# Row-tiled max scores, rounds of eight heads in the second pass, and a ring of two for the route weights of the last experts

## Chip, cores and metric

One core of one Trainium2 chip runs the whole program. The metric is the device time in microseconds (us) of one execution; three executions are shown for the kernel before, and one more was profiled.

## The reference

The program is a two-layer Perceiver block on x (256 tokens x 512) with a context of 4096 rows x 512. Each layer is cross attention to the context, self attention, and a mixture of experts, each with a residual. The change touches the second layer's cross attention (int8-rounded queries, 16 heads of 32) and its experts (32 experts, 8 per token). What these compute, cut to its core:

```python
# cross attention of layer 1: x -> queries, context -> keys and values
q = qdq(layernorm(x)) @ qdq(wq).T + bq          # 256 x 512, 16 heads of 32
k, v = split(ctx @ wkv.T + bkv)                 # 4096 x 512 each
o = softmax(q k^T / sqrt(32)) v                 # over the 4096 context rows
x = x + qdq(o) @ qdq(wp).T + bp
# experts of layer 1
scores = softmax(x @ wg.T); weights, idx = top_k(scores, 8); weights /= sum(weights)
h = silu(x_e @ w1[e]) * (x_e @ v1[e])           # 32 experts, hidden 192
out[t] += (h @ w2[e]) * weight[t, e]
```

## The kernel before

All tokens stay in SBUF (two tiles of 128 tokens, also kept transposed). The stages run one after the other, each in blocks that all engines enter and leave together; within a block the engines are ordered by semaphores alone, and each engine runs its list in order. Large products are made of three fp32r matmuls (high x high, low x high, high x low; the helper `product3`, L175 to L177).

**Cross attention, first pass** (stage_cross1, L1168 to L1346). The keys and values of the context are computed and the greatest score of each query is found, in 8 chunks k of 512 context rows. The work of TensorE for the next chunk is cut into 8 units (2 halves of 256 rows; in each, w = 0 and 1 make keys with 24 matmuls of 256 columns a unit, w = 2 and 3 make values with 12 matmuls of 512 columns), each unit into 4 quarters. Between two quarters stands one matmul of scores (L1278): for one head h and one tile t of 128 queries, `q_hi[:, h, tile]` (128 rows of which 32 hold the head's queries and 96 are zeros) against `keys_hi[:, u, h // 4, :]` (the keys of four heads on 128 rows), 512 columns, to one of the banks 0 to 3 in turn. VectorE takes the maximum of each (L1340), 32 in a chunk, and between them, at i = 1 and i = 18, splits the next context rows into high and low parts (`split`, L1326 and L1328). The matmul of turn i waits until the reduction four turns earlier is done. The last chunk has the 32 scores and no units. ScalarE takes keys and values out of PSUM (`take`), GpSimd makes the low part of the keys, SyncE stores keys in DRAM and loads context rows.

In the block before, `q_hi` is cleared by GpSimd (L1094) and filled by four copies of VectorE (L1122 to L1125), which are the last of its block; L1214 and the stores go on from `qT_hi` and `qT_lo`, the same queries with the heads of four on 128 rows.

**Second pass** (L1405 to L1532). For each of 32 tiles T of 128 context rows, TensorE makes the scores of 8 pairs p of heads (S, two matmuls a pair, L1513, to bank p % 4), ScalarE the exponentials of a pair (L1473), VectorE adds them up (L1459, pairs 0, 1, 4 to 7; pairs 2 and 3 are summed by TensorE, L1485), TensorE multiplies them with the values four pairs later (V, L1495). TensorE goes in rounds of two pairs: S of pairs p and p+1, then V of pairs p-4 and p-3. S of a pair waits for the exponential that used its bank. Stacked keys `k_stack` come from DRAM in two slots of two tiles each, three DMAs a slot (L1358), issued when the slot's last S is done.

**Experts** (stage_moe1, L1933 to L2198). The 32 experts are 16 pairs k. TensorE's order is up(0), up(1), down(0), up(2), down(1), and so on. The route weights are written to DRAM as 32 rows of 256 tokens and spread to all partitions in three groups of pairs, (0), (1 to 3), (4 to 15), into one tile `weight` of 16 pairs (load_weight, L1990 to L1997). SyncE issues them in one list with the expert weights: group 0, up(2, 0), group 1, up(2, 1), down(1), group 2, and then body(k) with up(k+3, 0), up(k+3, 1) and down(k+2). VectorE's `weigh` (L2154 to L2158) multiplies the hidden values with the weights and waits for the group once.

Of the kernel before, what the change touches and what calls it, by code (L numbers as in the profile page):

```python
# [1038 lines left out]
def stage_cross1(nc, g, A):  # L1039
    with ExitStack() as ctx:  # L1040
# [15 lines left out]
        q_hi = sb("q_hi", [P, Y_H, L], F32R, pass_scope)  # L1056
# [9 lines left out]
        with ExitStack() as c1:  # L1066
# [7 lines left out]
            (wq_loaded, wp_loaded, bias_loaded, pads_cleared, grid_step, x_rounded, wq_rounded,  # L1074
             wp_rounded, x_turned, w_turned, w_copied, x_copied, q_done, q_ready, split) = (sem(n) for n in (
                 "wq_loaded", "wp_loaded", "bias_loaded", "pads_cleared", "grid_step",
# [14 lines left out]
            with nc.Block() as block:  # L1091
                @block.gpsimd
                def _(pool):
                    pool.memset(q_hi[:, :, :].bitcast(F32), 0.0).then_inc(pads_cleared, 1)  # L1094
                    for c in range(NC):
                        kv.rest(pool, c)

                @block.vector
                def _(dve):
# [17 lines left out]
                    dve.wait_ge(pads_cleared, 1)  # L1117
# [54 lines left out]
        with ExitStack() as c2:  # L1172
# [20 lines left out]
            with nc.Block() as block:  # L1193
# [52 lines left out]
                def _(pe):  # L1246
# [40 lines left out]
                def _(act):  # L1287
# [22 lines left out]
                    def body(k, u, prep, more):  # L1310
                        if prep:
                            act.wait_ge(scores_ready, 32 * k + 1)
# [10 lines left out]
                def _(dve):  # L1323
# [7 lines left out]
                    def body(k, u, prep, more):  # L1331
                        for i in range(32):
# [6 lines left out]
                            dve.wait_ge(scores_ready, 32 * k + i + 1)  # L1339
# [62 lines left out]
        with ExitStack() as c4:  # L1402
# [18 lines left out]
            with nc.Block() as block:  # L1421
# [27 lines left out]
                def _(dve):  # L1449
                    def body(T, v, first, prep):  # L1450
                        for p in range(Y_PAIRS):
                            if p in PE_SUMS:
                                continue
                            dve.wait_ge(probs_ready, 8 * T + p + 1 + BANKS)
                            if first:
                                dve.tensor_copy(sums[:, p, :], probs[:, p, :]).then_inc(added, 1)
                                continue
                            dve.wait_ge(added, adds_before(T, p) + 1 - ADDS)
                            dve.tensor_tensor(sums[:, p, :], sums[:, p, :], probs[:, p, :], ALU.add).then_inc(added, 1)  # L1459
# [5 lines left out]
                def _(act):  # L1465
                    def body(T, v, first, prep):
                        for p in range(Y_PAIRS):
                            n = 8 * T + p
                            act.wait_ge(s_ready, n + 1)
                            act.wait_ge(pv_done, n + 1)  # L1470
                            if p not in PE_SUMS:
                                act.wait_ge(added, adds_before(T, p) + 1 - ADDS)
                            act.activation(probs[:, p, :], g.bank[p % BANKS][:, :], ACT.Exp).then_inc(probs_ready, 1)  # L1473
# [5 lines left out]
                def _(pe):  # L1479
# [22 lines left out]
                    def body(T, v, first, prep):  # L1502
# [3 lines left out]
                        for p in range(0, Y_PAIRS, 2):  # L1506

                            n = 8 * T + p
                            for b in range(2):
# [9 lines left out]
                            if p >= LAG or not first:  # L1519
                                pe.wait_ge(probs_ready, n - LAG + 2 + BANKS)  # L1520
                                for b in range(2):
# [410 lines left out]
def stage_moe1(nc, g, A):  # L1932
# [3 lines left out]
    with ExitStack() as ctx:  # L1936
# [15 lines left out]
        weight = sb("weight", [P, PAIRS, FC, L], F32)  # L1952
# [19 lines left out]
        weight_loaded = [sem(f"weight_loaded{n}") for n in range(3)]  # L1972
# [17 lines left out]
        def load_weight(sp, group):  # L1990
            k0, k1 = WEIGHT_GROUPS[group]
            pairs = route_dram[2 * k0:2 * k1, :].rearrange("(k j) n -> k j n", j=2)
            sp.dma_start(weight[:, k0:k1, 0:2, :],  # L1993
                         pairs.unsqueeze(0).to_broadcast([P, k1 - k0, 2, L])).then_inc(weight_loaded[group], 16)
            for j in range(2):
                sp.dma_start(weight[rows_of[j][1], k0:k1, 2, :],  # L1996
                             pairs[:, j, :].unsqueeze(0).to_broadcast([REST, k1 - k0, L])).then_inc(weight_loaded[group], 16)  # L1997

        WEIGHT_GROUPS = ((0, 1), (1, 4), (4, PAIRS))
# [17 lines left out]
        with nc.Block() as block:  # L2017
            @block.sync
            def _(sp):
# [6 lines left out]
                load_weight(sp, 0)  # L2026
                sp.wait_ge(gu_split, 3)
                load_up(sp, 2, 0)
                load_weight(sp, 1)
                sp.wait_ge(gu_split, 4)  # L2030
                load_up(sp, 2, 1)
                sp.wait_ge(dn_split, 1)
                load_down(sp, 1)
                load_weight(sp, 2)
# [310 lines left out]
```

## Time and profile before

| | |
|---|---|
| three executions | 1693.37 us median, 1692.62 to 1693.68 |
| the profiled execution | 1694.95 us, its span 1693.1 us |
| mean granted TensorE clock | 0.953 |
| TensorE matmul busy | 1555.1 us, 92% of the span |
| VectorE busy | 1122.3 us, 66% |
| ScalarE busy | 836.8 us, 49% |
| GpSimd busy | 214.4 us, 13% |

TensorE is busy in nearly every stretch. Busy time of a matmul runs from its issue to its end, and matmuls overlap, so what a matmul costs the queue is read from the distance between two starts, not from its own duration. PEclk is the granted clock as a share of full speed (1.00 is 2.4 GHz, 0.50 is 1.2 GHz).

### The profile page before, as it was taken

Reading aid. Unit: us, or ns where it says so; the run is one execution under the profiler, and the core shown is the slowest. Engines: PE = TensorE matmul, PEld = TensorE weight load, DVE = VectorE, ACT = ScalarE, POOL = GpSimd, SP = SyncE. Lnnn points to the kernel's source line nnn. Section 1 sums busy time; section 2 is a strip of 40 time slices with the busy share of each in tenths; the row PEclk is TensorE's granted clock in tenths of the full one; section 3 lists DMA queues with packets and bytes.
Section 4 is the critical chain, followed back from the end, with each engine's and each line's share of the span. In section 5 each row is a group of like instructions: output and inputs, shape, how many; then the busy total and the mean of one; then the engine's idle time right before and its main releaser. Section 6 shows DMA issues by size and latency. Waiting matters only on the chain. (4 is left out here: it accounts for less than half of the span.)

```text
span 1693.1 us, 35216 instructions
## 1 busy us (share of the span) xinstructions
PE 1555.1 (92%) x12406; PEld 1179.0 (70%) x12406; DVE 1122.3 (66%) x2206; ACT 836.8 (49%) x1429; POOL 214.4 (13%) x161
## 2 busy tenths in 40 slices
PE   5999999999979799999389999969999699869998
PEld 3667776777644499999378888835555455669997
DVE  5766666666524488887748888757776376556664
ACT  2677777777724444434122222228877066344553
POOL 0000000000013223323301111111110034000000
PEclk8999999999989799999689999959999799889999
DMA  3111111111020354442333332247774200485551
GB/s 131 45 37 39 41 38 39 37 37 43 1 106 1 138 180 178 164 165 97 124 87 113 112 111 101 74 88 147 144 144 93 81 1 1 147 279 196 180 187 68
DMA packets 74624, 169.13 MB, mean 100 GB/s; under 512 B 5442, under 2 KB 42098, under 8 KB 70963
## 3 DMA queue, kind: packets, MB, share of 16 engines
q1 hardware_dynamic: 74564, 168.35, 33.0%
q8 instruction: 35, 0.57, 0.1%
q14 instruction: 25, 0.20, 0.0%
HBM read 149.41 MB, written 17.33 MB: 98 GB/s over the span
## 5 line engine op out<-in xcount | busy, mean ns | idle before, releaser
L457 ACT ACTIVATE x_probs<-psum 128x1024 f32<-128x1024 f32 x256 | 248.3, 1022 | 12.9 <-PE psum L340 3.6
L175 PE MATMUL psum<-m_x_hi,m_gu_hi 128*128 128x256 f32 (+1 forms) x816 | 233.7, 286 | 15.3 <-DVE m_h L2152 12.8
L176 PE MATMUL psum<-m_x_hi,m_gu_lo 128*128 128x256 f32 (+1 forms) x816 | 232.6, 285 | 0.0
L177 PE MATMUL psum<-m_x_lo,m_gu_hi 128*128 128x256 f32 (+1 forms) x816 | 232.2, 285 | 0.0
L175 PE MATMUL psum<-x_w_hi,x_ctx_hi 128*128 128x256 f32 (+1 forms) x640 | 208.7, 326 | 10.8 <-DVE x_ctx_lo L484 10.8
L1340 DVE TENSOR_REDUCE x_peaks<-psum 128x512 f32 (+1 forms) x256 | 169.0, 687 | 44.2 <-PE psum L1278 43.9
L176 PE MATMUL psum<-x_w_hi,x_ctx_lo 128*128 128x256 f32 (+1 forms) x640 | 195.0, 305 | 0.0
L177 PE MATMUL psum<-x_w_lo,x_ctx_hi 128*128 128x256 f32 (+1 forms) x640 | 194.6, 304 | 0.0
L175 PEld LDWEIGHTS psum<-x_w_hi,x_ctx_hi 128*128 128x128 f32 x640 | 121.5, 190 | 68.1 <-issue 52.1
L175 PEld LDWEIGHTS psum<-m_x_hi,m_gu_hi 128*128 128x128 f32 (+1 forms) x816 | 153.6, 188 | 18.2 <-DVE m_h L2152 13.4
L1473 ACT ACTIVATE x_probs<-psum 128x512 f32<-128x512 f32 x256 | 138.8, 595 | 34.9 <-PE psum L1513 33.0
L176 PEld LDWEIGHTS psum<-m_x_hi,m_gu_lo 128*128 128x128 f32 (+1 forms) x816 | 153.6, 188 | 1.2
L177 PEld LDWEIGHTS psum<-m_x_lo,m_gu_hi 128*128 128x128 f32 (+1 forms) x816 | 153.7, 188 | 0.0
L1459 DVE TENSOR_TENSOR x_sums<-x_sums,x_probs 128x512 f32<-128x512 f32 x186 | 118.9, 688 | 50.5 <-ACT x_probs L1473 50.5
L349 PE MATMUL psum<-x_probs,x_vals 128*17 128x256 f32 x2048 | 135.4, 382 | 0.0
L176 PEld LDWEIGHTS psum<-x_w_hi,x_ctx_lo 128*128 128x128 f32 x640 | 122.3, 191 | 5.4 <-issue 0.2
L177 PEld LDWEIGHTS psum<-x_w_lo,x_ctx_hi 128*128 128x128 f32 x640 | 122.1, 191 | 5.3
L1829 DVE TENSOR_TENSOR m_gu_lo<-m_gu_raw,m_gu_hi 128x704 fp32r<-128x704 f32 x72 | 105.5, 1489 | 24.8 <-ACT m_gu_hi L1723 24.8
L1513 PEld LDWEIGHTS psum<-x_q_stack,x_k_stack 97*128 97x128 f32 x512 | 70.2, 193 | 63.0 <-ACT x_probs L1473 51.1
L1278 PE MATMUL psum<-x_keys_hi,x_q_hi 128*128 128x512 f32 x256 | 105.6, 429 | 0.9
L1513 PE MATMUL psum<-x_q_stack,x_k_stack 97*128 97x256 f32 x512 | 96.9, 313 | 10.2 <-ACTq L1475 10.2
L519 DVE COPY x_keysT<-psum 128x1024 f16<-128x1024 f16 x64 | 44.2, 690 | 83.4 <-PE psum L330 83.0
(298 smaller groups left out, 3024.7 us busy)
## 6 DMA issues: line engine op xcount, KB each, us to landing
m_gu_raw<-in_m_gu SPq DMA_DIRECT2D x18, 1408.0 KB, 5.9
x_k_stack<-x_keys_dram SPq DMA_DIRECT2D x48, 512.0 KB, 7.3
m_gu_raw<-in_m_gu SPq DMA_DIRECT2D x32, 768.0 KB, 4.1
x_ctx_raw<-in_ctxT SPq DMA_DIRECT2D x64, 256.0 KB, 2.6
m_dn_raw<-in_m_down SPq DMA_DIRECT2D x16, 768.0 KB, 4.1
m_dn_raw<-in_m_down SPq DMA_DIRECT2D x18, 512.0 KB, 3.8
x_ctx_raw<-in_ctxT SPq DMA_DIRECT2D x16, 512.0 KB, 3.8
x_keys_dram<-x_keys_hi SPq DMA_DIRECT2D x16, 512.0 KB, 3.2
```

The lines of the kernel that those rows point to most:

```text
L175: pe.matmul(out, a[0], b[0], start=start, stop=False, skip_group_check=True)
L176: pe.matmul(out, a[1], b[0], start=False, stop=False, skip_group_check=True)
L177: return pe.matmul(out, a[0], b[1], start=False, stop=stop, skip_group_check=True)
L349: last = pe.matmul(acc[grp // 2][32 * q:32 * q + XHD + 1, (grp % 2) * L:(grp % 2 + 1) * L], vals[:, s % 2, 4 * grp + q, :], probs[:, grp, ...
L457: act.activation(probs[:, grp, :], g.psum[:, 2 + 2 * (grp % 2):4 + 2 * (grp % 2), :].rearrange("p b n -> p (b n)"), ACT.Exp).then_inc(prob ...
L519: dve.tensor_copy(keysT[:, s % 2, :, :].rearrange("p a n -> p (a n)"), turn_bank.bitcast(F16)).then_inc(keys_ready, 1)
L1278: pe.matmul(g.bank[i % BANKS][:, :], q_hi[:, h, t * P:(t + 1) * P], keys_hi[:, u, h // 4, :], start=True, stop=True).then_inc(scores_ready, 1)
L1340: dve.tensor_reduce(peaks[:, i % 2, i // 2, bass.ds(k, 1)], g.bank[i % BANKS][:, :], AX, ALU.max).then_inc(scores_read, 1)
L1459: dve.tensor_tensor(sums[:, p, :], sums[:, p, :], probs[:, p, :], ALU.add).then_inc(added, 1)
L1473: act.activation(probs[:, p, :], g.bank[p % BANKS][:, :], ACT.Exp).then_inc(probs_ready, 1)
L1513: last = pe.matmul(g.bank[(p + b) % BANKS][:, a * L:(a + 1) * L], k_stack[0:ROWS, s, h, u * P:(u + 1) * P], q_stack[0:ROWS, h, :], start=T ...
L1829: dve.tensor_tensor(gu_lo[:, u, c, :], gu_raw[:, u, c, :], gu_hi[:, u, c, :].bitcast(F32), ALU.subtract).then_inc(gu_split, 1)
```

## The change

Three edits, in different stages.

1. First pass: a round is now one m (four heads) and one t. Four matmuls of 32 rows each, on partitions 32j to 32j+31 of `qT_hi` and `keys_hi`, write banks 0 to 3; one reduction of 128 x (4 x 512) takes all four. There are 8 rounds in a chunk, each followed by a whole unit, and a round waits for the reduction of the round before it. `q_hi`, its clearing and its four copies are gone. The splits of VectorE stand before rounds 1 and 5.
2. Second pass: rounds of four pairs in place of two; the exponentials and the additions are made for two pairs in one instruction.
3. Experts: `weight` holds two pairs; the rows of pair k are spread by four DMAs into slot k % 2; those of pairs 0 and 1 before up(2, 0) is issued, those of pair k+2 in body(k), after down(k+2) and a wait for the weighing of pair k.

```diff
-                    pool.memset(q_hi[:, :, :].bitcast(F32), 0.0).then_inc(pads_cleared, 1)
...
-                    hi = q_hi[:, :, :].rearrange("p (m j) n -> p m j n", j=4)
-                    for j in range(4):
-                        r = slice(32 * j, 32 * j + 32)
-                        dve.tensor_copy(hi[r, :, j, :], qT_hi[r, :, :])
...
-                        for i in range(2 * UNITS * STEPS):
-                            h, t = i // 2, i % 2
-                            pe.wait_ge(scores_read, 32 * k + i + 1)
-                            pe.matmul(g.bank[i % BANKS][:, :], q_hi[:, h, t * P:(t + 1) * P],
-                                      keys_hi[:, u, h // 4, :], start=True, stop=True).then_inc(scores_ready, 1)
+                        for i in range(NC * NT):
+                            m, t = i // NT, i % NT
+                            pe.wait_ge(scores_read, NC * NT * k + i + 1)
+                            for j in range(BANKS):
+                                rows = slice(32 * j, 32 * j + 32)
+                                last = pe.matmul(g.bank[j], qT_hi[rows, m, t * P:(t + 1) * P], keys_hi[rows, u, m, :],
+                                                 start=True, stop=True)
+                            last.then_inc(scores_ready, 1)
                             if prep:
-                                s, w, quarter = i // 16, i // 4 % 4, i % 4
-                                unit(2 * k + 2 + s, s, w, quarter)
+                                for quarter in range(STEPS):
+                                    unit(2 * k + 2 + i // UNITS, i // UNITS, i % UNITS, quarter)
...
-                            if more and i == 18:
+                            if more and i == 5:
...
-                            dve.tensor_reduce(peaks[:, i % 2, i // 2, bass.ds(k, 1)], g.bank[i % BANKS][:, :], AX,
-                                              ALU.max).then_inc(scores_read, 1)
-
-                    dve.sem_inc(scores_read, BANKS)
+                            dve.tensor_reduce(peaks[:, t, 4 * m:4 * m + 4, bass.ds(k, 1)].rearrange("p h k -> p (h k)"),
+                                              g.psum[:, 0:BANKS, :], AX, ALU.max).then_inc(scores_read, 1)
+
+                    dve.sem_inc(scores_read, 1)
...
-                            dve.tensor_tensor(sums[:, p, :], sums[:, p, :], probs[:, p, :], ALU.add).then_inc(added, 1)
+                            dve.tensor_tensor(sums[:, two, :], sums[:, two, :], probs[:, two, :],
+                                              ALU.add).then_inc(added, 2)
...
-                            act.activation(probs[:, p, :], g.bank[p % BANKS][:, :], ACT.Exp).then_inc(probs_ready, 1)
+                            act.activation(probs[:, p:p + 2, :], g.psum[:, p % BANKS:p % BANKS + 2, :],
+                                           ACT.Exp).then_inc(probs_ready, 2)
...
-                        for p in range(0, Y_PAIRS, 2):
+                        for p in range(0, Y_PAIRS, LAG):
 
                             n = 8 * T + p
-                            for b in range(2):
+                            for b in range(LAG):
                                 pe.wait_ge(probs_ready, n + b + 1)
...
-        weight = sb("weight", [P, PAIRS, FC, L], F32)
+        weight = sb("weight", [P, 2, FC, L], F32)
...
+        def load_weight(sp, k, u):
             for j in range(2):
+                row = route_dram[bass.ds(2 * k + j, 1), :]
+                sp.dma_start(weight[:, u, j, :], row.to_broadcast([P, L])).then_inc(weight_loaded[u], 16)
+                sp.dma_start(weight[rows_of[j][1], u, 2, :],
+                             row.to_broadcast([REST, L])).then_inc(weight_loaded[u], 16)
...
+                load_weight(sp, 0, 0)
+                load_weight(sp, 1, 1)
+                for j in range(2):
+                    sp.wait_ge(gu_split, j + 3)
+                    load_up(sp, 2, j)
                 sp.wait_ge(dn_split, 1)
                 load_down(sp, 1)
-                load_weight(sp, 2)
...
                         load_down(sp, k + 2)
+                        sp.wait_ge(scaled, k + 1)
+                        load_weight(sp, k + 2, u)
```

## Rows read from the trace of the kernel before

**Rows 1.** Windows: engines' busy us (instructions), granted clock, DMA share, GB/s.

```profile
1240.00:1260.00 20.00, 20.00 (x211) 11.17 (x205) 14.38 (x23) 16.06 (x30) 1.94 (x4) 1.00 0.76 143
1510.00:1520.00 10.00, 8.87 (x59) 8.87 (x60) 8.58 (x10) 6.56 (x9) 0.00 (x0) 0.74 0.69 240
1543.00:1556.00 13.00, 13.00 (x94) 12.18 (x93) 8.77 (x10) 6.62 (x8) 0.00 (x0) 1.00 0.52 181
```

**Rows 2.** Timeline, block before the first pass: start, us, engine, work, idle before.

```profile
824.20 3.51 POOL L1094 MEMSET x_q_hi<- 128x4096 f32 x1 [3.94 <-POOLq L89]
825.83 2.55 DVE L1027 TENSOR_SCALAR x_norm<-x_norm,x_per_grid 128x512 f32<-128x512 f32 x2
...
848.94 1.66 DVE L1027 TENSOR_SCALAR x_wp<-x_wp,x_per_grid 128x512 f32<-128x512 f32 x4
...
861.25 2.77 DVE L1125 CAST x_q_hi<-x_qT_hi 32x1024 fp32r<-32x1024 f32 x4
```

**Rows 3.** Timeline of PE in the middle of the first pass.

```profile
956.91 0.40 PE L1278 MATMUL psum<-x_keys_hi,x_q_hi 128*128 128x512 f32 x1
957.15 0.28 PE L175 MATMUL psum<-x_ctx_hi,x_w_hi 128*128 128x256 f32 x1
...
957.86 0.40 PE L1278 MATMUL psum<-x_keys_hi,x_q_hi 128*128 128x512 f32 x1
...
961.78 0.39 PE L175 MATMUL psum<-x_w_hi,x_ctx_hi 128*128 128x512 f32 x1
...
962.46 0.39 PE L1278 MATMUL psum<-x_keys_hi,x_q_hi 128*128 128x512 f32 x1
```

**Rows 4.** Timeline of DVE in the same stretch.

```profile
957.45 0.69 DVE L1340 TENSOR_REDUCE x_peaks<-psum 128x512 f32 x1 [0.26 <-PE psum L1278]
...
967.27 0.69 DVE L1326 CAST x_ctx_hi<-x_ctx_raw 128x1024 fp32r<-128x1024 f32 x1
...
969.13 3.07 DVE L1340 TENSOR_REDUCE x_peaks<-psum 128x512 f32 x5
```

**Rows 5.** Timeline of PE and DVE, last chunk of the first pass.

```profile
1099.52 18.11 PE L1278 MATMUL psum<-x_keys_hi,x_q_hi 128*128 128x512 f32 x32
1099.95 19.22 DVE L1340 TENSOR_REDUCE x_peaks<-psum 128x1 f32<-128x512 f32 x32 [0.22 <-PE psum L1278]
```

**Rows 6.** The line of the max scores: durations ns min/median/max, first and last start.

```profile
L1278 PE MATMUL psum<-x_keys_hi,x_q_hi x256: 387/396/796, 890.5 to 1116.8; 128*128 128x512 f32 x128
```

**Rows 7.** Timeline of PE in the first layer's cross attention, tiles of the array.

```profile
302.35 0.61 PE L340 MATMUL psum<-x_q_rows,x_keysT 64*128 64x256 f16 x8
302.89 1.06 PE L349 MATMUL psum<-x_probs,x_vals 128*17 128x256 f32 x16
```

**Rows 8.** Timeline of PE in the second pass, one context tile.

```profile
1204.25 0.74 PE L1513 MATMUL psum<-x_q_stack,x_k_stack 97*128 97x256 f32 x4
1204.91 0.64 PE L1495 MATMUL psum<-x_probs,x_v_now 128*32 128x256 f32 x8
1205.48 0.75 PE L1513 MATMUL psum<-x_q_stack,x_k_stack 97*128 97x256 f32 x4
...
1207.98 0.75 PE L1513 MATMUL psum<-x_q_stack,x_k_stack 97*128 97x256 f32 x4
...
1209.65 0.74 PE L1513 MATMUL psum<-x_q_stack,x_k_stack 97*128 97x256 f32 x4
```

**Rows 9.** Timeline of ACT in the same tile.

```profile
1204.87 2.24 ACT L1473 ACTIVATE x_probs<-psum 128x512 f32<-128x512 f32 x4 [0.59 <-PE psum L1513]
```

**Rows 10.** The page, costliest groups: an exponential over two banks, 1024 columns.

```profile
L457 ACT ACTIVATE x_probs<-psum 128x1024 f32<-128x1024 f32 x256 | 248.3, 1022 | 12.9 <-PE psum L340 3.6
```

**Rows 11.** Timelines of SP, ACT and PE, first pairs of the last experts.

```profile
1478.53 13.42 SPq L1996 DMA_DIRECT2D m_weight<-m_route_dram  x2
...
1507.35 1.48 ACT L2055 ACTIVATE m_gu_hi<-m_gu_raw 128x1536 fp32r<-128x1536 f32 x1 [13.72 <-DMA m_gu_raw<-in_m_gu]
...
1511.13 0.58 PE L175 MATMUL psum<-m_x_hi,m_gu_hi 128*128 128x256 f32 x1 [11.91 <-DVE m_h L2152]
```

More of the change, by code:

```diff
@@ L1055, in stage_cross1 @@
         pass_scope = ExitStack()
-        q_hi = sb("q_hi", [P, Y_H, L], F32R, pass_scope)
         qT_hi = sb("qT_hi", [P, NC, L], F32R, pass_scope)
@@ L1073, in stage_cross1 @@
             grid = sb("grid", [P, 16], F32, c1)
-            (wq_loaded, wp_loaded, bias_loaded, pads_cleared, grid_step, x_rounded, wq_rounded,
+            (wq_loaded, wp_loaded, bias_loaded, grid_step, x_rounded, wq_rounded,
              wp_rounded, x_turned, w_turned, w_copied, x_copied, q_done, q_ready, split) = (sem(n) for n in (
-                 "wq_loaded", "wp_loaded", "bias_loaded", "pads_cleared", "grid_step",
+                 "wq_loaded", "wp_loaded", "bias_loaded", "grid_step",
                  "x_rounded", "wq_rounded", "wp_rounded", "x_turned", "w_turned", "w_copied", "x_copied",
@@ L1311, in body @@
                         if prep:
-                            act.wait_ge(scores_ready, 32 * k + 1)
+                            act.wait_ge(scores_ready, NC * NT * k + 1)
                             for s in range(2):
@@ L1331, in body @@
                     def body(k, u, prep, more):
-                        for i in range(32):
+                        for i in range(NC * NT):
+                            m, t = i // NT, i % NT
                             if prep and i == 1:
@@ L1450, in body @@
                     def body(T, v, first, prep):
-                        for p in range(Y_PAIRS):
+                        for p in range(0, Y_PAIRS, 2):
                             if p in PE_SUMS:
                                 continue
-                            dve.wait_ge(probs_ready, 8 * T + p + 1 + BANKS)
+                            two = slice(p, p + 2)
+                            dve.wait_ge(probs_ready, 8 * T + p + 2 + BANKS)
                             if first:
-                                dve.tensor_copy(sums[:, p, :], probs[:, p, :]).then_inc(added, 1)
+                                dve.tensor_copy(sums[:, two, :], probs[:, two, :]).then_inc(added, 2)
                                 continue
-                            dve.wait_ge(added, adds_before(T, p) + 1 - ADDS)
-                            dve.tensor_tensor(sums[:, p, :], sums[:, p, :], probs[:, p, :], ALU.add).then_inc(added, 1)
+                            dve.wait_ge(added, adds_before(T, p) + 2 - ADDS)
+                            dve.tensor_tensor(sums[:, two, :], sums[:, two, :], probs[:, two, :],
+                                              ALU.add).then_inc(added, 2)
                     dve.sem_inc(added, ADDS)
@@ L1466, in body @@
                     def body(T, v, first, prep):
-                        for p in range(Y_PAIRS):
+                        for p in range(0, Y_PAIRS, 2):
                             n = 8 * T + p
-                            act.wait_ge(s_ready, n + 1)
-                            act.wait_ge(pv_done, n + 1)
+                            act.wait_ge(s_ready, n + 2)
+                            act.wait_ge(pv_done, n + 2)
                             if p not in PE_SUMS:
-                                act.wait_ge(added, adds_before(T, p) + 1 - ADDS)
-                            act.activation(probs[:, p, :], g.bank[p % BANKS][:, :], ACT.Exp).then_inc(probs_ready, 1)
+                                act.wait_ge(added, adds_before(T, p) + 2 - ADDS)
+                            act.activation(probs[:, p:p + 2, :], g.psum[:, p % BANKS:p % BANKS + 2, :],
+                                           ACT.Exp).then_inc(probs_ready, 2)
                     act.sem_inc(probs_ready, BANKS)
@@ L1519, in body @@
                             if p >= LAG or not first:
-                                pe.wait_ge(probs_ready, n - LAG + 2 + BANKS)
-                                for b in range(2):
+                                pe.wait_ge(probs_ready, n + BANKS)
+                                for b in range(LAG):
                                     if p >= LAG:
@@ L1971, in stage_moe1 @@
              "route_ready", "route_turned", "route_taken", "route_stored"))
-        weight_loaded = [sem(f"weight_loaded{n}") for n in range(3)]
+        weight_loaded = [sem(f"weight_loaded{n}") for n in range(2)]
         gu_loaded = [sem("gu_loaded0"), sem("gu_loaded1")]
@@ L2155, in weigh @@
                     dve.wait_ge(h_ready, 4 * k + 8)
+                    dve.wait_ge(weight_loaded[u], 64 * (k // 2 + 1) if isinstance(k, int) else 32 * k + 64 - 32 * u)
                     dve.tensor_tensor(hw[:, :, :], h[:, :, :],
-                                      weight[:, bass.ds(k, 1), :, :].rearrange("p k f n -> p (k f) n"),
-                                      ALU.mult).then_inc(scaled, 1)
+                                      weight[:, u, :, :], ALU.mult).then_inc(scaled, 1)
                 def split_hidden(k, u):
```

19 lines of the change are left out of this document (1 added, 18 removed).

## The prediction

> **What bounds the kernel now.** I read the windows first: in the middle of the second pass and in the steady part of the experts TensorE is busy for the whole stretch at the full clock, the DMA engines for 0.76 and 0.52 of it, while the pairs just before the experts' steady part still have TensorE idle and the mean clock at 0.74 [rows 1]. Then the timelines of TensorE, where the distance of two starts tells what a matmul costs its queue. In the first pass there is no hole: six matmuls of 256 columns take 957.15 to 957.86, 0.118 us each, three of 512 columns take 961.78 to 962.46, 0.227 each, and a matmul of max scores costs 0.24, as much as any other of 512 columns although 96 of its 128 rows are zeros [rows 3]. VectorE waits there for the scores [rows 4]. So in both passes TensorE's queue sets the time. Two places are bound otherwise: the last chunk of the first pass, where VectorE reduces without a hole, 32 reductions in 19.22 us [rows 5], and the first pairs of the last experts, where TensorE sits idle for 11.91 us [rows 11].
>
> **Part 1a, block before the first pass: -4.4 us.** The four copies into `q_hi` end that block, 2.77 us, and go [rows 2]. The clearing of `q_hi` on GpSimd runs 824.20 to 827.71; two TENSOR_SCALARs of VectorE that start at 825.83 take 2.55 us, where four of the same size take 1.66 later on, so two should take about 0.85: 1.7 us were lost to the clearing [rows 2]. VectorE's chain ends the block, so both go off the time: 2.77 + 1.7 = 4.4 (range 2.8 to 4.5, if a load is late next).
>
> **Part 1b, seven chunks with units: -16 us.** A chunk now takes (1099.52 - 890.5) / 7 = 29.86 us [rows 5, 6]. Its units alone take 4 x 24 x 0.118 to 0.120 + 4 x 12 x 0.227 = 22.3 us [rows 3], the 32 scores 7.5. After the change there are 8 rounds. That tiles of the array on different rows run side by side is shown by the first layer's scores: eight matmuls of 256 columns on 64 rows each take 302.35 to 302.89, 0.54 us [rows 7], against 8 x 0.107 = 0.86 by the length of 256 columns at 2.4 GHz; two at a time would be 0.43, and 0.11 is left, which I read as 0.09 for changing the layout of the array and a little for the weights. A round is then: change 0.09, weights that nothing hides 0.11, 512 columns 0.227, change back 0.09, and again exposed weights 0.11, in all about 0.63. The 0.11 comes from the second pass: S of four takes 1204.25 to 1204.91, 0.66, where four at the pitch of 0.118 are 0.47 and 0.09 is the change [rows 3, 8]. For four tiles at once no row stands; bounds are 0.63 (all four together) and 0.40 + 4 x 0.227 = 1.31 (one after the other), and I take the lower, nearest to the 64-row case, where tiles shared the time wholly.
>
> The new wait: a round waits for the reduction of the round before, and a whole unit stands in between. From the start of a score matmul to the reduction it frees takes 956.91 to 957.45, 0.54 us [rows 3, 4], plus 0.11 for the exposed weights. The reduction of 4 x 512: one of 512 takes 0.69 but back to back 0.61 (5 in 3.07) [rows 4]; with 1536 more elements at 0.53 per 512 it is 2.29. With 0.05 to release TensorE the loop is 0.65 + 2.29 + 0.05 = 2.99, the round with its unit 2.8 + 0.63 = 3.43. So the wait is over before TensorE arrives, by 0.4. Twice in a chunk a split stands before a reduction, 967.27 to 969.13, 1.86 us [rows 4]: it makes that reduction end 4.07 + 2.99 = 7.06 after the start of the round before (0.65 + 2.21 + 1.86 + 2.29 + 0.05), where two rounds with units of keys take 2 x (2.87 + 0.63) = 7.0. That is 0.1 of a stall each time. Queued behind the split is only that reduction, behind the wait on TensorE the next four tiles. A chunk: 22.3 + 8 x 0.63 + 0.2 = 27.5, 2.3 less, times 7 = -16.1.
>
> **Part 1c, last chunk: +6 us.** With no unit to hide it the loop sets the pace, and TensorE, mostly waiting, falls to half the clock there already now: the longest of these matmuls takes 0.796 [rows 6]. A turn: 0.80 + 0.14 + 2.29 + 0.05 = 3.27, eight of them 26.1, a little less in the first, 25.7; now it is 1099.52 to 1119.17, 19.65 [rows 5]. Before, four banks let matmuls run under the reductions. Cost +6.0 (range +4 to +7.5).
>
> **Part 2, second pass: -13 us.** Now a tile T takes 1204.25 to 1209.65, 5.40 [rows 8]: four S of 0.66, three V of 0.57, and one V with sums, 1209.65 - 1207.98 - 0.66 = 1.01. The pitches are spent on matmuls and on changes between layouts; half of the changes go. S of eight is 0.66 + 4 x 0.118 = 1.14, V of eight 0.57 + 0.43 = 1.00 (0.43 is what V with sums has more for its second four), V with sums 1.44. Sum 2 x 1.14 + 1.00 + 1.44 = 4.72. But the banks are four and a round now fills all four. The first exponential starts 0.62 after its S [rows 8, 9], for two pairs 0.86; over two banks one lasts 1.02 [rows 10], and its pitch I put at 0.92, since the reductions' pitch too is some 0.1 under their length. So the second ends at 0.86 + 0.92 + 1.02 = 2.80. TensorE comes to the first S that needs those banks at 1.14 + 1.00 + 0.34 = 2.48 and waits until 2.86. The other half has V with sums in front and no wait. T = 4.72 + 0.38 less what the restart overlaps, 4.97 to 5.1; I take 4.98. 32 x 0.43 = 13.8 saved, less 1.0 at the end, where the last exponential and the last addition are of double length: -12.8 (range -9 to -21: the wait full, or none). VectorE and ScalarE have room: 3 additions of 1.22 and 4 exponentials of 0.92. The keys: the DMA engines work for 0.76 of the time at 5.40 a tile [rows 1]; at 4.98 this is 0.82, so transfers don't bind, but they come closer.
>
> **Part 3, last experts: -14 us.** SyncE's list now holds the third group of weights: its two last issues alone take 13.42 us of the queue [rows 11], and up(3) stands behind them. ScalarE waits 13.72 us for that load and TensorE 11.91 [rows 11]. Afterwards a stretch of 10 us has a mean clock of 0.74 [rows 1], which costs 2.6 less the part in which TensorE is idle anyway, 2.0. Small waits of TensorE before it, behind the same transfers, I put at 1. After the change eight short DMAs stand before up(2, 0), some 4 us of issue for now 1.5; up(2) then comes 1 to 2 us later, and the first weighing 0.5, while down(0) hides the former. The later four DMAs a pair are some 2 us of SyncE and 0.4 MB in 12.9 us at a DMA share of 0.52 [rows 1]; TensorE's work covers them, and if that cover failed it would cost up to 1 us a pair. Sum: 11.9 + 2.0 + 1.0 - 0.5 = 14.4, taken as -14.0 (range -10 to -16).
>
> **Sum.** -4.4 - 16.1 + 6.0 - 12.8 - 14.0 = -41.3. The profiled execution took 1694.95 (its span 1693.1), so it would be 1653.6; it stands 1.6 over the median of 1693.37, which gives 1652.1 for the median. I forecast 1652.
>
> **A figure of the Trainium skill.** The Trainium skill, "TensorE: Matmul & The Clock Gate", section "Measured speedup vs the span model", gives 3.07 times for four row tiles with 512 columns, not 4; by that the round is 0.07 longer, part 1b 4 us less, and the time 1656. No row here has four row tiles.
>
> **The rivals.**
> A, the tiles run one after the other, and the kernel is slower. The place is the four matmuls of a round. For it: with fp32r and four row groups there is no row; against it: the 64-row tiles [rows 7]. A round is 1.31 and a chunk 22.3 + 10.5 = 32.8, +2.9 x 7 = +20.6 in place of -16.1; in the last chunk three more times 0.43 at half the clock, eight times, +10.2. 1652 + 36.7 + 10.2 = 1699. It decides from a round of 0.94 on, where part 1b gives nothing; all parts together turn positive at about 1.25.
> B, they run two by two, as on 64 rows: a round 0.86, 0.23 x 56 + 0.43 x 8 = +16: 1668.
> C, the reduction sets the pace. If one over four banks costs 4 x 0.69 = 2.76 the loop is 3.46, over the round, and the splits come on top in full: a chunk 8 x 3.46 + 3.7 = 31.4, +27, and +4 in the last chunk: 1683. For it: no reduction over several banks is in the trace; against it: the 0.61 back to back shows that most of the 0.69 goes by elements. The Trainium skill, "TensorEngine Tiling (Array Packing)", section "PSUM Bottleneck", warns that after tiling PSUM evacuation may become the bottleneck: that is this rival, and in the last chunk it is in my sum.
> D, the second pass gives little, because a full set of banks makes S and exponentials take turns more than reckoned, or keys come late: part 2 at -3, 1662.
> E, the experts gain half, because the short DMAs or their issues delay other loads: part 3 at -6, 1660.
> F, no wait in the second pass and no stall in the first: 1643.
>
> **How the numbers follow.** Forecast with its own spread (1645 to 1658) 0.58; A 0.05; B 0.10; C 0.07; D 0.07; E 0.06; F 0.07. The range 1641 to 1670 takes in the forecast, B, D, E and F. About 0.2% (3.4 us) is what a measurement of this kernel can tell from no change. Slower by more than that: the upper part of A, 0.04, and 0.02 for a mishap not listed; within it 0.03; faster 0.91.
>
> **What would show it.** Right: in the first pass the starts of the four score matmuls of a round within some 0.02 us of each other and rounds of 3.4; reductions of 2.3 us; the last chunk some 26 us; tiles of the second pass at about 5.0 with a hole of 0.4 before the third pair of every second S; in the experts no idle of TensorE over 2 us before the steady part, and a period of 12.85 as before. Wrong: score matmuls 0.2 apart (A), reductions near 2.8 (C), TensorE waiting for key loads (D), ScalarE waiting for expert loads (E).

## The result, and the profile after

| | before | after |
|---|---|---|
| median | 1693.53 us (1692.62 to 1694.08) | 1663.94 us (1661.08 to 1664.97) |
| the profiled execution, its span | 1694.95, 1693.1 | 1664.54, 1663.0 |
| granted clock | 0.953 | 0.951 |

The ratio is 0.9823, interval 0.9806 to 0.984: 29.6 us or 1.8% less. 1652 was forecast with a range of 1641 to 1670, so the direction and the range hold, and the gain is 0.7 of the forecast one (41.3). But 1663.9 lies above 1645 to 1658, the spread that the forecast gave to its own sum; it is inside the range only because the range leaves room for rivals.

The page of after has for its reductions, its two-bank exponentials and its additions (busy, mean ns, idle before and releaser):

```profile
L1337 DVE TENSOR_REDUCE x_peaks<-psum 128x2048 f32 (+1 forms) x64 | 146.7, 2291 | 56.9 <-PE psum L1273 56.9
...
L1472 ACT ACTIVATE x_probs<-psum 128x1024 f32<-128x1024 f32 x128 | 124.1, 1022 | 36.9 <-PE psum L1513 36.4
L1457 DVE TENSOR_TENSOR x_sums<-x_sums,x_probs 128x1024 f32<-128x1024 f32 x93 | 111.5, 1227 | 45.9 <-ACT x_probs L1472 44.6
```

Where the time went is best read by stretches, cut at instructions that both kernels have. Each number is the difference of two starts in the timelines, in us: SyncE's first load of the second layer's cross attention, the first max reduction, VectorE's first instruction after the last one, the first load after the second pass, and the first load of the last experts' stage.

| stretch | before | after | difference | forecast |
|---|---|---|---|---|
| all before the second layer's cross attention | 818.0 | 818.9 | +0.9 | 0 |
| to the first reduction (part 1a) | 73.1 | 72.1 | -1.0 | -4.4 |
| first pass (parts 1b, 1c) | 228.4 | 218.3 | -10.1 | -10.1 |
| second pass with its entry (part 2) | 190.1 | 179.3 | -10.8 | -12.8 |
| to the last experts, code unchanged | 139.3 | 140.9 | +1.6 | 0 |
| last experts (part 3) | 244.1 | 233.5 | -10.6 | -14.0 |

The 0.9 in the first row is not the change's: in the twelve profiled executions of this document the same code takes between 816.2 and 818.9 us there.

**First pass.** The timeline of PE and DVE in after, lines 176 and 177 left out, answers to [rows 3] and [rows 4]:

```profile
934.83 0.68 DVE L1322 CAST x_ctx_hi<-x_ctx_raw 128x1024 fp32r<-128x1024 f32 x1
...
935.46 0.51 PE L1273 MATMUL psum<-x_keys_hi,x_qT_hi 32*128 32x512 f32 x4
935.54 1.23 DVE L1324 TENSOR_TENSOR x_ctx_lo<-x_ctx_raw,x_ctx_hi 128x1024 fp32r<-128x1024 f32 x1
...
936.68 2.29 DVE L1337 TENSOR_REDUCE x_peaks<-psum 128x2048 f32 x1
...
939.02 0.51 PE L1273 MATMUL psum<-x_keys_hi,x_qT_hi 32*128 32x512 f32 x4
939.47 0.50 PE L175 MATMUL psum<-x_w_hi,x_ctx_hi 128*128 128x512 f32 x1
939.70 2.29 DVE L1337 TENSOR_REDUCE x_peaks<-psum 128x2048 f32 x1 [0.73 <-PE psum L1273]
...
942.41 0.50 PE L1273 MATMUL psum<-x_keys_hi,x_qT_hi 32*128 32x512 f32 x4
942.85 0.50 PE L175 MATMUL psum<-x_w_hi,x_ctx_hi 128*128 128x512 f32 x1
943.08 2.29 DVE L1337 TENSOR_REDUCE x_peaks<-psum 128x2048 f32 x1 [1.09 <-PE psum L1273]
```

The line of the scores by itself (ns min/median/max), against [rows 6]:

```profile
L1273 PE MATMUL psum<-x_keys_hi,x_qT_hi x256: 488/497/792, 890.3 to 1105.8; 32*128 32x512 f32 x128
```

The four score matmuls of a round start within 0.01 us of each other and together last 0.51 us where one lasts 0.50, and the next matmul starts 0.45 after them, where four in a row would hold it up by 4 x 0.227 = 0.91: they run side by side. A round is 942.41 - 939.02 = 3.39; over the seven chunks a round with a unit of values takes 3.35 to 3.42, one with a unit of keys 3.48 to 3.51, and up to 3.59 where its reduction stands behind a split. The reduction at 936.68 is such a one and ends at 938.97; the scores follow at 939.02, 0.05 later. In the chunks with units TensorE waits for VectorE at these rounds and nowhere else.

The last chunk, timeline of DVE in after, against [rows 5]:

```profile
1090.63 2.29 DVE L1337 TENSOR_REDUCE x_peaks<-psum 128x4 f32<-128x2048 f32 x1 [0.91 <-PE psum L1273]
1093.84 2.29 DVE L1337 TENSOR_REDUCE x_peaks<-psum 128x4 f32<-128x2048 f32 x1 [0.91 <-PE psum L1273]
```

Here VectorE waits 0.91 us in each round of 3.2 (the first two rounds, still at full clock, are 2.91), where before it had no hole.

**Second pass.** Timeline of PE, and the waits between 1130 and 1280 us (us in total, times, longest), in after, against [rows 8]:

```profile
1205.35 1.22 PE L1513 MATMUL psum<-x_q_stack,x_k_stack 97*128 97x256 f32 x8
1206.49 1.07 PE L1495 MATMUL psum<-x_probs,x_v_now 128*32 128x256 f32 x16
1207.49 1.50 PE L1513 MATMUL psum<-x_q_stack,x_k_stack 97*128 97x256 f32 x8
1208.92 0.84 PE L1495 MATMUL psum<-x_probs,x_v_now 128*32 128x256 f32 x10
...
1210.36 1.21 PE L1513 MATMUL psum<-x_q_stack,x_k_stack 97*128 97x256 f32 x8
```

```profile
DVE x_sums L1457 <- ACT x_probs L1472: 43.6, 57, 3.1
ACT x_probs L1472 <- PE psum L1513: 35.4, 60, 2.6
PEld psum L1513 <- ACT x_probs L1472: 30.4, 86, 0.4
```

A tile is 1210.36 - 1205.35 = 5.01. One group of S passes in 1.14, its V in 1.00, as added up in part 2; the other takes 1.43, 0.29 more: weights for S wait for the exponentials. The start of the pass is different. Tiles 0 and 1 begin, before (first two lines) and after, at

```profile
1132.02 0.76 PE L1513 MATMUL psum<-x_q_stack,x_k_stack 97*128 97x256 f32 x2 [10.24 <-ACTq L1475]
1139.08 0.91 PE L1513 MATMUL psum<-x_q_stack,x_k_stack 97*128 97x256 f32 x3
```

```profile
1121.62 1.62 PE L1513 MATMUL psum<-x_q_stack,x_k_stack 97*128 97x256 f32 x6 [10.07 <-ACTq L1475]
1130.05 1.15 PE L1513 MATMUL psum<-x_q_stack,x_k_stack 97*128 97x256 f32 x6
```

so the first tile, at half clock in both, takes 8.43 us for 7.06; the second takes 5.18 for 5.69.

**Last experts.** Timelines of SP, ACT and PE in after, against [rows 11]:

```profile
1453.26 0.34 SPq L1993 DMA_DIRECT2D m_weight<-m_route_dram  x1
...
1457.21 0.47 SPq L1994 DMA_DIRECT2D m_weight<-m_route_dram  x1
1457.72 1.06 SPq L1985 DMA_DIRECT2D m_gu_raw<-in_m_gu  x2
...
1464.45 1.49 ACT L2051 ACTIVATE m_gu_hi<-m_gu_raw 128x1536 fp32r<-128x1536 f32 x1 [4.19 <-DMA m_gu_raw<-in_m_gu]
...
1468.23 0.48 PE L175 MATMUL psum<-m_x_hi,m_gu_hi 128*128 128x256 f32 x1 [2.39 <-DVE m_h L2148]
```

The 11.91 us of idle TensorE are gone, and so are the two issues of 13.42. But eight short DMAs take SyncE from 1453.26 to 1457.7, the weights of up(2) land late (ScalarE waits 4.19), and TensorE waits 2.39: up(2) starts 38.7 us after the stage's first load, for 35.4 before. Of the ten us from 1464, 3.4 are at half clock (mean 0.83), and up(2) takes 10.2 us where each later pair takes 8.6. Windows of after; the last three columns are clock, DMA share and GB/s.

```profile
1461.00:1464.00 3.00, 2.61 (x11) 2.18 (x12) 0.24 (x1) 0.00 (x0) 0.00 (x0) 1.00 1.00 394
1464.00:1474.00 10.00, 7.61 (x43) 6.91 (x42) 7.55 (x8) 6.11 (x8) 0.00 (x0) 0.83 0.76 273
```

### The profile page after: what moved, and what is told of

Same layout as the page of the kernel before. It is cut to its first block and busy times, and to the rows that moved or that the text cites. A ratio compares the mean times of both kernels' runs of the same rounds, so it can differ in the third digit from the quotient of the medians.

```text
span 1663.0 us, 34177 instructions
## 1 busy us (share of the span) xinstructions
PE 1519.6 (91%) x12406; PEld 1150.2 (69%) x12406; DVE 1087.9 (65%) x1914; ACT 821.9 (49%) x1301; POOL 233.6 (14%) x160
## 5 line engine op out<-in xcount | busy, mean ns | idle before, releaser
L457 ACT ACTIVATE x_probs<-psum 128x1024 f32<-128x1024 f32 x256 | 248.2, 1022 | 12.9 <-PE psum L340 3.7
L175 PE MATMUL psum<-x_w_hi,x_ctx_hi 128*128 128x256 f32 (+1 forms) x640 | 212.1, 331 | 10.8 <-DVE x_ctx_lo L484 10.8
L1337 DVE TENSOR_REDUCE x_peaks<-psum 128x2048 f32 (+1 forms) x64 | 146.7, 2291 | 56.9 <-PE psum L1273 56.9
L1472 ACT ACTIVATE x_probs<-psum 128x1024 f32<-128x1024 f32 x128 | 124.1, 1022 | 36.9 <-PE psum L1513 36.4
L1457 DVE TENSOR_TENSOR x_sums<-x_sums,x_probs 128x1024 f32<-128x1024 f32 x93 | 111.5, 1227 | 45.9 <-ACT x_probs L1472 44.6
L1513 PE MATMUL psum<-x_q_stack,x_k_stack 97*128 97x256 f32 x512 | 87.5, 305 | 12.5 <-ACTq L1475 10.1
L1776 POOL TENSOR_TENSOR m_dn_lo<-m_dn_raw,m_dn_hi 128x1024 fp32r<-128x1024 f32 (+1 forms) x36 | 75.1, 2086 | 155.2 <-ACT m_dn_hi L1728 153.8
```

The lines of the kernel that those rows point to most:

```text
L175: pe.matmul(out, a[0], b[0], start=start, stop=False, skip_group_check=True)
L457: act.activation(probs[:, grp, :], g.psum[:, 2 + 2 * (grp % 2):4 + 2 * (grp % 2), :].rearrange("p b n -> p (b n)"), ACT.Exp).then_inc(prob ...
L1337: dve.tensor_reduce(peaks[:, t, 4 * m:4 * m + 4, bass.ds(k, 1)].rearrange("p h k -> p (h k)"), g.psum[:, 0:BANKS, :], AX, ALU.max).then_in ...
L1457: dve.tensor_tensor(sums[:, two, :], sums[:, two, :], probs[:, two, :], ALU.add).then_inc(added, 2)
L1472: act.activation(probs[:, p:p + 2, :], g.psum[:, p % BANKS:p % BANKS + 2, :], ACT.Exp).then_inc(probs_ready, 2)
L1513: last = pe.matmul(g.bank[(p + b) % BANKS][:, a * L:(a + 1) * L], k_stack[0:ROWS, s, h, u * P:(u + 1) * P], q_stack[0:ROWS, h, :], start=T ...
```

## The experiments

The kernel before was timed again beside each group of variants, with medians of 1693.5 to 1694.7 us; ratios are against it. Differences between two variants below 2 us are read from the stretches, not from the medians. P is in each case the explanation drawn from the two traces above, and the other letter its rival.

**Each part alone.** The edits are those of the diff above, part by part.

> The kernel before with the edits of the first pass alone (row-tiled max scores, no q_hi). Theory P, read off the two traces: seven chunks give 7 x (29.85 - 27.66) = 15.4 us, the last chunk costs 5.2, the block before gives about 1, because the earlier projection falls into half clock: -11 us, 1682. Rival Q, the block before gives the 4.4 us that were forecast and only the chip's luck hid them in the profiled execution: -14.5 us, 1679.

Measured: 1682.94 us, ratio 0.9934 (0.9917 to 0.995), 11.3 less. To the first reduction 71.9, first pass 218.2 us. This is P: the block before gives 1.2 and not 4.4 here as well.

> The kernel before with the rounds of eight heads alone. Theory P: a tile takes 5.01 in place of 5.40 us, 32 of them, a little lost at the end: -12 to -12.5 us, 1681. Rival R, the gain depends on the stages in front (keys in DRAM, clock at the entry): under -9 or over -15.

Measured: 1685.21 us, ratio 0.9951 (0.9934 to 0.9967), 9.0 less, a miss by P and on the edge of R. But the second pass itself has 178.8 us, 11.4 less, with tiles of 5.00, so P is right about the tile, and the gain does not depend on the stages in front; 1.3 us come back in the unchanged stretch behind it (140.6 for 139.3), which neither had.

> The kernel before with the ring of two for the route weights alone. Theory P: TensorE's idle 11.9 us of the third pair goes, the second pair comes 3.3 us later behind eight short DMAs: -10 to -11 us, 1683. Rival S, the profiled execution met the half clock by chance in the second pair: -12.5 to -14 us. If P and the other two hold, the three gains add up to 33 us against 29.6 measured together within the noise of 2 us; a larger gap would show that the parts influence each other.

Measured: 1683.11 us, ratio 0.9937 (0.9921 to 0.9954), 11.1 less; the experts' stretch is 233.3. This is P, and up(2) takes 10.2 us here too, so the half clock in that pair is no chance. The three gains sum to 31.3 against 29.6 in the whole, within the noise of 2 us. The clock's share doesn't add up, though: the first pass alone and the second pass alone each lengthen the unchanged stretch by 1.3, both together by 1.6.

**Exponentials of one bank.** Of the kernel after:

```diff
-                        for p in range(0, Y_PAIRS, 2):
+                        for p in range(Y_PAIRS):
...
-                            act.activation(probs[:, p:p + 2, :], g.psum[:, p % BANKS:p % BANKS + 2, :],
-                                           ACT.Exp).then_inc(probs_ready, 2)
+                            act.activation(probs[:, p, :], g.bank[p % BANKS][:, :], ACT.Exp).then_inc(probs_ready, 1)
```

> The kernel after, with ScalarE making the exponentials one pair (one bank, 512 columns) at a time again; rounds of eight heads and double additions stay. Theory P: the 0.3 us that TensorE waits in every tile comes from the two-bank exponential that holds the third pair's bank until 2.8 us; with single ones that bank is free at 2.2 us and a tile takes 4.72 to 4.80 us: -7 to -9 us against the kernel after, 1656. Rival T, the wait comes from four banks being too few, whatever the size of the exponentials: a tile stays at 5.0 us and the time at 1664, or worse, as ScalarE has 8 x 0.49 = 3.95 in place of 3.7 us of work.

Measured: 1652.68 us, ratio 0.9747 (0.9729 to 0.9765); the second pass with its entry falls from 179.3 to 169.1. Timeline of PE:

```profile
1199.76 1.20 PE L1512 MATMUL psum<-x_q_stack,x_k_stack 97*128 97x256 f32 x8
...
1202.32 1.21 PE L1512 MATMUL psum<-x_q_stack,x_k_stack 97*128 97x256 f32 x8
1203.46 1.07 PE L1494 MATMUL psum<-x_probs,x_v_now 128*32 128x256 f32 x16
1204.46 1.20 PE L1512 MATMUL psum<-x_q_stack,x_k_stack 97*128 97x256 f32 x8
```

Both groups of S now last 1.20, the tile is 1204.46 - 1199.76 = 4.70, and T falls: four banks are enough. The gain is larger than P's 7 to 9. ScalarE's work rises (8 instructions of 0.60 for 4 of 1.02) and the kernel gets faster, since the third bank comes free 0.65 us sooner (2.20 us after the start of S, for 2.85). Some 2.4 us of the gain are the first tile, 6.05 for 8.43, of which a part is the clock, which rises earlier there: in the run with all four edits below, where it rises nearly as late as in after, the first two tiles take 12.2 for 13.6. On the other side four of the later tiles are longer than 4.75, the longest 5.43, and TensorE has waits of 0.6 and 1.1 us for keys. With shorter tiles the loads of the keys begin to show, which they don't in after.

**Order of the route weights.** Of the kernel after:

```diff
                 load_weight(sp, 0, 0)
-                load_weight(sp, 1, 1)
                 for j in range(2):
                     sp.wait_ge(gu_split, j + 3)
                     load_up(sp, 2, j)
                 sp.wait_ge(dn_split, 1)
                 load_down(sp, 1)
+                load_weight(sp, 1, 1)
```

> The kernel after with one change of order in SyncE's list: the weights of pair 1 are issued behind up(2, 0), up(2, 1) and down(1), not in front of them. Theory P: up(2) is late because eight short DMAs stand before it (5.0 us of issue, landing at 1464.36, 34.9 us after the stage's first issue); with four in front TensorE's start of up(2) moves forward by about 2.5 us, and the stretch at half clock that the hole caused (1.6 us) goes too: -3 to -4 us against the kernel after, 1660.5. Rival U, something else than the order holds up(2) (ScalarE's list, the DMA engines' rate): within 1 us of 1664.

Measured: 1659.95 us, ratio 0.9792 (0.9776 to 0.9808). The experts' stretch is 230.5 for 233.5, 3.0 less: P. Timeline of SP: up(2) is issued behind four short DMAs.

```profile
1453.04 0.52 SPq L1994 DMA_DIRECT2D m_weight<-m_route_dram  x1
1453.60 1.06 SPq L1985 DMA_DIRECT2D m_gu_raw<-in_m_gu  x2
1454.70 0.43 SPq L1988 DMA_DIRECT2D m_dn_raw<-in_m_down  x1
```

Up(2) starts 37.3 us after the stage's first load for 38.7; these are 1.4 (P had 2.5), and the other 1.6 are the half clock that no longer follows: up(2) takes 8.6 us for 10.2.

**Two sets of banks in the last chunk.** Of the kernel after; `at` is also the first bank that the reduction reads:

```diff
-                            pe.wait_ge(scores_read, NC * NT * k + i + 1)
+                            at = 0 if prep else BANKS * (i % 2)
+                            pe.wait_ge(scores_read, NC * NT * k + (i if prep or i == 0 else i - 1) + 1)
+                            if at and i == 1:
+                                pe.wait_ge(unit_taken, UNITS * 2 * CHUNKS + UNITS)
...
-                                last = pe.matmul(g.bank[j], qT_hi[rows, m, t * P:(t + 1) * P], keys_hi[rows, u, m, :],
+                                last = pe.matmul(g.bank[at + j], qT_hi[rows, m, t * P:(t + 1) * P], keys_hi[rows, u, m, :],
```

> The kernel after, with the last chunk of the first pass writing its rounds in turn to banks 0 to 3 and 4 to 7, which are free there. Theory P: the last chunk is bound by matmul, handover and reduction one after the other (3.20 us a round); with two sets the reduction alone sets the pace, 2.2 us: eight rounds in 18 us in place of 25.5, -7 us, 1657. Rival V, the reduction itself is slowed by TensorE's writes or by the lower clock: rounds of 2.7 or more, -3 us or less.

Measured: 1655.51 us, ratio 0.9762 (0.9746 to 0.9778), the first pass 211.5 for 218.3, 6.8 less: P. Timeline of DVE, eight reductions without a hole:

```profile
1082.92 17.68 DVE L1341 TENSOR_REDUCE x_peaks<-psum 128x4 f32<-128x2048 f32 x8 [1.09 <-PE psum L1276]
```

**The clock in the block before.** The first edit adds matmuls that nobody reads; the second puts back the clearing and the four copies of `q_hi`, as in the kernel before, also unread.

```diff
+                    for _ in range(48):
+                        pe.matmul(g.bank[3], g.zeros[:, 0:P], g.zeros[:, :], start=True, stop=True)
                     turn(wq, wq_rounded)
```

> The kernel after with 48 more matmuls of zeros on TensorE, whose result is not used, in the 14 us before the projection of the queries, where it idles. Theory P: the forecast's 3.4 us too much in the block before the first pass were lost to TensorE's half clock (the projection of 32 matmuls takes 9.33 us after and 7.17 before); at full clock it takes 7.0: -2 to -3.5 us, 1661. Rival W, the gain was lost elsewhere (loads, VectorE's port): no change.

Measured: 1659.66 us, ratio 0.9785 (0.9769 to 0.9802); to the first reduction 68.5 for 72.1: P.

> The kernel after, with the clearing and the four copies of q_hi put back though nobody reads it. Theory P: the two cost VectorE 4.4 us of its chain, but the projection then starts after the clock has risen: the stage is longer by 1 us only, 1665. Rival W: it is longer by the whole 4.4 us, 1668.

Measured: 1659.94 us, ratio 0.9789 (0.9772 to 0.9805); to the first reduction 73.4 for 72.1, 1.2 more, as P has it for the stretch. But the whole got 3.6 to 4.0 us faster (1659.9 for 1663.9 and, in a repetition below, 1663.5), which neither theory had: the unchanged stretch has 140.0 for 140.9 and the experts 230.7 for 233.5. In the experts the half clock falls on down(0), while the weights of up(2) are still on their way, and not on up(2), which takes 8.7 us for 10.2. That is half of it, and the other half is at the end. Windows of the last matmuls in after (first line) and here (second; clock in the last column but two): the same work meets another clock. Why it falls elsewhere the runs don't show.

```profile
1652.00:1657.00 5.00, 4.82 (x14) 3.85 (x15) 0.04 (x1) 0.00 (x0) 0.00 (x0) 0.66 0.00 0
```

```profile
1650.00:1655.00 5.00, 4.45 (x18) 3.31 (x18) 0.36 (x2) 0.00 (x0) 0.00 (x0) 1.00 0.00 0
```

The timelines show the same for the block before. The projection of the queries (32 matmuls) and the transposes in front of it (16) in after, in the run with zeros, and with the pads kept:

```profile
845.22 3.67 PE L1134 MATMUL psum<-ident,x_wq 128*128 128x128 f32 x16 [14.10 <-DVEq L1104]
849.58 9.33 PE L1143 MATMUL psum<-x_xqT,x_wqT 128*128 128x256 f32 x32 [0.69 <-ACT x_wqT L1160]
```

```profile
844.01 1.97 PE L1134 MATMUL psum<-ident,x_wq 128*128 128x128 f32 x16 [2.65 <-DVEq L1104]
846.82 7.17 PE L1145 MATMUL psum<-x_xqT,x_wqT 128*128 128x256 f32 x32 [0.84 <-ACT x_wqT L1162]
```

```profile
846.61 3.67 PE L1141 MATMUL psum<-ident,x_wq 128*128 128x128 f32 x16 [14.10 <-DVEq L1106]
850.97 7.17 PE L1150 MATMUL psum<-x_xqT,x_wqT 128*128 128x256 f32 x32 [0.69 <-ACT x_wqT L1167]
```

All start after 14 us in which TensorE idled, but for the run with zeros. In after the work comes 1.7 us earlier (the transposes 26.4 us after the stage's first load, for 28.05), and it meets the half clock for longer and takes 2.16 longer. Windows of 845 to 850 and 850 to 855 us, before (first two lines) and after:

```profile
845.00:850.00 5.00, 3.67 (x16) 3.27 (x16) 4.85 (x18) 2.06 (x4) 0.00 (x0) 0.54 0.00 0
850.00:855.00 5.00, 4.61 (x21) 4.09 (x22) 3.52 (x10) 0.34 (x1) 0.00 (x0) 1.00 0.00 0
```

```profile
845.00:850.00 5.00, 4.10 (x17) 3.70 (x18) 4.85 (x18) 2.39 (x4) 0.00 (x0) 0.50 0.00 0
850.00:855.00 5.00, 5.00 (x15) 4.01 (x15) 2.71 (x8) 0.00 (x0) 0.00 (x0) 0.60 0.00 0
```

Before, the clock rises just short of 850, in front of the projection at 850.39; in after it rises at about 854, 4 us into the projection at 849.58. All twelve profiled executions agree: with the transposes at 28.05 the projection takes 7.17 us (four of them), at 26.4 it takes 9.2 to 9.3 (six), and behind the zeros 7.17 (two).

**All together.**

> The kernel after, unchanged, on the chip of the combination. Theory: the block before the first pass gains only about 1 us because its clock rises late, whatever execution is profiled; 1664 (1661 to 1666). If the clock's steps were the chance of one profiled execution, the stretch from the first issue to the first reduction would come out 3 us shorter here and the median below 1661.

Measured: 1663.53 us, ratio 0.9814 (0.9801 to 0.9828). The stretches are 72.1, 218.3, 179.3, 140.9 and 233.5, each within 0.1 us of those shown above. The clock's steps are not the luck of one execution.

> The kernel after with all four edits: exponentials of one bank, weights of pair 1 later, two sets of banks in the last chunk, 48 more matmuls before the projection. The four lie in different stretches, so by theory their stage gains add up: 10.2 + 3.1 + 6.8 + 3.7 = 23.8 us less than the kernel after, 1640. If they interfere (keys of the second pass late at a shorter tile, or the clock's steps falling badly) it stays above 1645.

Measured: 1638.21 us, ratio 0.9667 (0.9653 to 0.9681), 25.3 less than the kernel after beside it, 56.5 less than before. The stretches: 68.4, 211.6, 170.1, 139.6, 230.0. 1640 was expected. The gains of the four stages add up (23.1 us for 23.8), and 1.3 us more come from the unchanged stretch.

## Why the prediction was right, and where not

**Part 1b** held: a chunk was reckoned at 27.5 us and takes 27.66 in the mean, its round with its unit 3.43 and 3.35 to 3.51, the reduction 2.29 and 2.29, the loop after a split 7.06 and 7.07. The lower bound and the nearest row (64-row tiles, [rows 7]) led to the right end: rivals A, B and C have no trace left. What a round adds to its units was 0.63 and is 0.65. In all the seven chunks give 15.4 for 16.1.

**Part 1c** held in kind and is 0.7 too high: 3.20 us a round for 3.27, and 2.91 in the first two, which are still at full clock; 5.3 for 6.0. That the loop of matmul, handover and reduction is what it costs is shown by the two sets of banks, which take off 6.8, more than the cost. That the first pass came out at its forecast 10.1 exactly is luck: the two misses of 0.7 cancel.

**Part 2**: the wait at the third pair of every second S was foreseen at 0.38 and is 0.29; the tile is 5.01 for 4.98, since the overlap that the forecast took off the wait isn't there. The cause, the two-bank exponential that gives back its banks late, is shown by its removal. What failed is the term for the ends. It was 1.0 at the last tile; the end costs 0.2, but the first two tiles take 13.6 us for 12.75 before, where the forecast had them 0.9 shorter. Some of that is half clock and some the double exponentials, and the runs don't part the two. With 0.40 saved in a tile for 0.43, it makes 10.8 for 12.8. (The forecast's own 5.40 and 4.98 differ by 0.42, so its 13.8 should have been 13.4.) Rival D was not it: 10.8 and not 3, and no wait for keys stands in the waits.

**Part 3**: the mechanism was right (11.91 us of idle TensorE gone, and up(3) at full clock, 8.6 us for 10.5), the size 3.4 too high. The failed step is "up(2) then comes 1 to 2 us later, while down(0) hides the former". It comes 3.3 later, and nothing hides that: eight issues take 4.4 us, its weights land 4.2 us after ScalarE is ready. The sum had 0.5 for it. Behind this new hole of 2.39 us the half clock came back for 1.6, so that the 1.0 of small waits was not gained either. This is the mechanism of rival E, with ScalarE waiting for a load as its sign, at less than half of E's size (10.6, for 6 by E and 14 by the forecast); the sign "no idle of TensorE over 2 us before the steady part" was missed with 2.39. The later four DMAs a pair cost nothing: the period is 12.85 as before. Order alone returns 3.0.

**Part 1a**: the step that failed is "both go off the time". Both did go: the two TENSOR_SCALARs take 0.87 for 2.55 us, and the copies are gone. But TensorE stood at half clock when the earlier work reached it, and the projection took 9.33 for 7.17 us, 2.2 of the missing 3.4. The other 1.2 are of the same kind, one step on. The first keys and values start at 866.42 before and at 865.09 in after,

```profile
866.42 0.58 PE L175 MATMUL psum<-x_ctx_hi,x_w_hi 128*128 128x256 f32 x1 [7.11 <-DVE x_ctx_lo L1328]
```

```profile
865.09 0.58 PE L175 MATMUL psum<-x_ctx_hi,x_w_hi 128*128 128x256 f32 x1 [4.44 <-DVE x_ctx_lo L1324]
```

and their matmuls come 0.21 us apart until 870.0 and until 871.0, then 0.12: 5.9 us at half clock for 3.6. The zeros, which stand in front of all this, leave that second part as it is. The forecast took TensorE's clock from where the work stood in the trace of before, and never asked at what clock the work would run that it moved. The clock is behind the 1.6 us of the unchanged stretch too: windows of its first 40 us have a mean clock of 0.74 before (1309.60 on) and 0.70 after (1288.50 on).

```profile
1309.60:1349.60 40.00, 25.10 (x73) 15.37 (x74) 11.82 (x30) 3.86 (x7) 2.66 (x5) 0.74 0.25 92
```

```profile
1288.50:1328.50 40.00, 24.88 (x66) 15.33 (x67) 11.91 (x30) 3.86 (x7) 2.65 (x5) 0.70 0.24 92
```

0.04 of 40 us are 3.2 us more at half clock, or 1.6 us of work. Why the clock rises where it does there was not settled; that it is the clock and not the code is, since code and work are the same.

The terms then: 3.4 (part 1a), 2.0 (part 2), 3.4 (part 3), 1.6 (unchanged stretch) and 0.9 before the stage are 11.3 us, all to one side; the profiled span of 1663.0 is 11.2 over what the sum makes of the span before, 1651.8.

The Trainium skill's 3.07 for four row tiles ("TensorE: Matmul & The Clock Gate", "Measured speedup vs the span model") would have added 0.07 to a round, 0.70 for 0.63. Here a round adds 0.65, and the four last 0.51 together where one lasts 0.50. The Trainium skill's warning on PSUM evacuation ("TensorEngine Tiling (Array Packing)", "PSUM Bottleneck") came true in the last chunk alone, where no other work of TensorE stands beside the reduction.

## What to carry to other kernels

A larger instruction saves starts but holds its banks longer: ask which matmul waits for the first of them, and let the consumer work in the smallest piece that the producer waits for. Where a ring replaces one large transfer, put in front of the critical load only what is needed before it. And when work is moved earlier behind a stretch in which TensorE idles, price it at half clock: 48 matmuls of zeros there were worth 3.6 us, more than the 1.0 that removing the work had brought.

## What the runs showed of the hardware

- Four fp32r matmuls on 32 rows each run side by side, 0.51 us for four of 512 columns, at a price of 0.65 us of TensorE's queue for the round with both changes of the array's layout.
- A reduction over four banks takes 2.29 us, 0.53 for each 512 columns beyond the 0.69 of the first; whether a part of that is the crossing of a bank isn't shown.
- A spread of one row to 128 or 64 partitions keeps SyncE for 0.34 to 0.59 us in front of up(2), as long as the issue of a 768 KB load (0.33 to 0.58), so eight of them (64 or 128 KB each) hold up the next load by 4.4 us.
- Putting 4.4 us of useless work of VectorE and GpSimd back into one block made the whole kernel some 3 us faster (span 1659.6 for 1663.0 and 1662.5): 1.2 more in its own stretch, and less in stages that it doesn't touch, where the same work met the full clock.
